# Three float16 products for each float32 projection, and a later first lag product, in a one-core attention and feed-forward kernel

## Chip, cores and metric

The kernel runs on one core of one Trainium2 chip. The metric is the device time of the whole program in microseconds (us), the median of several executions.

## What is computed

The input is x, 4096 rows of 256 channels. Cut to what matters here:

```python
q, k, v = split(layernorm(x) @ Wqkv_w + Wqkv_b)           # 3 x 256 channels, 16 heads of 16
y_softmax = softmax(causal(q @ k.T * scale)) @ v
# a recurrence over all rows, for every head
state = retention * state + Gamma * (v_t outer k_t);  y_t = (W_static + state) @ q_t
g = gelu(layernorm(x) @ gate_w1 + gate_b1)                # 128 channels
alpha = sigmoid(g @ gate_w2 + gate_b2)
x = x + (alpha * y_softmax + (1 - alpha) * y_stp) @ out_w + out_b
x = x + ffn_fp8(layernorm(x))
```

## The kernel before

The kernel has three parts, each a block in which every engine has a program of its own. The engines meet through semaphores, each waits in its own order, and an engine that waits holds up all that stands behind the wait.

**The prologue** makes everything that depends on x alone. x is taken in 8 chunks of 512 rows. For a chunk, VectorE finds mean and variance (`moments`, L830 to L838), GpSimd raises the variance to the power -1/2 (`power`, L584), VectorE normalises (`normalise`, L846), TensorE turns the result so that channels lie on partitions (`turn`, L685), ScalarE copies the turned columns out of PSUM as float32 (`columns`, L769, tile `xn_t`), and TensorE multiplies (`project`, L700): 7 units of 128 output channels (two each for q, k and v, one for the gate), each the sum of two float32 matmuls of 128x128 by 128x512. The units alternate between PSUM banks 2 and 3, so unit u+2 waits until ScalarE has emptied the bank of unit u (`products`, L776, L780, and L785 for the gate's gelu). After that VectorE splits q and k into two float16 parts (`split`, L856 and L858), TensorE turns v back (`turn_back`, L713) and makes the gate's logits (L720), and SyncE (SP) stores all of it in DRAM (`store`, L505, L511, L515) and loads the next x (`next_x`, L497). TensorE's order is project(c), turn(c+1), turn_back(c). VectorE's order, from chunk 0 on, is split(c), moments(c+2), normalise(c+2); for the last chunks it is moments and normalise of chunk c+1, then the maxima of the next paragraph, then split(c).

From chunk 5 on, a first piece of the next part is mixed in: TensorE makes scores of q and k for the first query chunk, pair by pair (`first_maxima`, L664 and L669), between units 2 and 3 of chunk 5 and units 0 to 3 of chunks 6 and 7, and VectorE takes their row maxima (L954). They need q and k of chunks 0 to 3 read back from DRAM: SP waits until these are stored (L560), loads them (L529 and L537) and only then stores chunk 4. The other 22 of the 32 pairs follow behind chunk 7.

At the very start VectorE squares Wqkv (L864), TensorE sums the squares (L728), and a chain of small VectorE instructions with one GpSimd power in it (L599) makes a scale for each channel, to `chan_bias` (L892). Between normalise(1) and split(0) VectorE has a setup chain: constants of the recurrence, and the fp8 rounding of the feed-forward weight (L897 to L946). It waits once for GpSimd's `partition_all_reduce` of one number (L620), behind which GpSimd fills two large tiles (L622, L624).

**The attention part** starts when all engines have left the prologue. Its order of work is written out in a list; `first_steps` (L170) is its beginning: the maxima of the second query chunk (L1232 on TensorE, L1433 on VectorE), 40 pairs through four PSUM banks, and, when 8 single maxima of them have been issued, the first lag product (L1306), a matmul that waits for a GpSimd product `kq` (L1123). **The last part** merges, projects and applies the feed-forward layer.

Of the kernel before, what the change touches and what calls it, by code (L numbers as in the profile page):

```python
# [8 lines left out]
I32 = mybir.dt.int32  # L9
# [26 lines left out]
SHIFT_UNIT = 2.0 ** 15  # L36
SCALE = HD ** -0.5
# [60 lines left out]
N_WEIGHTS = 12  # L98
# [70 lines left out]
def first_steps():  # L169
# [167 lines left out]
def preln_attention_ffn_kernel(nc, x, wqkv, bqkv, out_w, out_b, w_static, lam, gamma, gate_w1,  # L337
                               gate_b1, gate_w2, gate_b2, ffn_wt, ffn_b, out):
    ctx = ExitStack()
    with ctx:  # L340
# [56 lines left out]
        xnt_evac = free_sem("xnt_evac", 2)  # L397
# [61 lines left out]
        with pro:  # L459
# [26 lines left out]
            xn_t = sb("xn_t", [P, 2, HALF, CH], where=pro)  # L486
# [6 lines left out]
            with nc.Block() as block:  # L493
                @block.sync
                def _(sp):
# [46 lines left out]
                    def copy_sides():  # L542
                        sp.wait_ge(pool_setup, 13)
# [36 lines left out]
                def _(pool):  # L580
# [12 lines left out]
                    pool.wait_ge(pool_setup, 5)  # L593
                    power(1)

# [8 lines left out]
                    pool.wait_ge(pool_setup, 8)  # L604
# [7 lines left out]
                    pool.wait_ge(pool_setup, 11)  # L612
# [10 lines left out]
                    pool.wait_ge(pool_setup, 13)  # L623
# [25 lines left out]
                def _(pe):  # L649
# [26 lines left out]
                    pe.wait_ge(pool_setup, 3)  # L676
                    pe.wait_ge(first_weights, 16 * 2)
# [11 lines left out]
                    def project(it, par, between=()):  # L689
# [40 lines left out]
                    mm.then_inc(bounds_ready, 1)  # L730
                    turn(0, 0)
                    pe.wait_ge(weights_loaded, 16 * N_WEIGHTS)
# [16 lines left out]
                def _(act):  # L749
                    for dst, src in [(wqkv_sb[:, :, :], wqkv.rearrange("(c p) n -> p c n", p=P)), (bqkv_sb[:, :], bqkv)]:  # L750
                        act.dma_start(dst, src).then_inc(first_weights, 16)
                    for dst, src in [
                            (w1_sb[:, :, :], gate_w1.rearrange("(c p) n -> p c n", p=P)),
# [10 lines left out]
                    def columns(it, par):  # L764
                        for c in range(HALF):
# [3 lines left out]
                            act.activation(xn_t[:, par, c, :], PS[:, c, :], ACT.Identity).then_inc(xnt_evac, 1)  # L769

                    def products(it, par):

                        act.wait_ge(stored[par], it * STORES_PER_CHUNK + STORES_PER_CHUNK)
                        for u in range(4):
                            act.wait_ge(proj_ready, it * 14 + par * 7 + u + 15)
                            act.activation(proj[:, par, u, :], PS[:, PROJ_BANK + u % 2, :], ACT.Identity,  # L776
                                           bias=chan_bias[:, u:u + 1], scale=chan_scale[:, u:u + 1]).then_inc(proj_evac, 1)
                        for u in range(4, 6):
                            act.wait_ge(proj_ready, it * 14 + par * 7 + u + 15)
                            act.activation(proj[:, par, u, :], PS[:, PROJ_BANK + u % 2, :], ACT.Identity,  # L780
                                           bias=bqkv_sb[:, u:u + 1]).then_inc(proj_evac, 1)
# [3 lines left out]
                        act.activation(gate_t[:, par, :], PS[:, PROJ_BANK + (UNITS_PER_CHUNK - 1) % 2, :], ACT.Gelu, bias=b1_sb[:, 0:1])\  # L785
# [14 lines left out]

                    act.wait_ge(weights_loaded, 16 * N_WEIGHTS)
                    act.activation(lam_sb[:, :], lam_sb[:, :], ACT.Exp, scale=-1.0).then_inc(act_setup, 1)
                    columns(0, 0)

                    act.wait_ge(vaug_ready, 2)
                    act.wait_ge(scales_ready, 7)
# [16 lines left out]
                def _(dve):  # L823
# [26 lines left out]
                    def split(it, par):  # L850
# [10 lines left out]

                    moments(0, 0)
                    dve.wait_ge(first_weights, 16 * 2)
                    dve.tensor_tensor(w_square[:, :, :], wqkv_sb[:, :, 0:2 * D], wqkv_sb[:, :, 0:2 * D], ALU.mult)\  # L864
                        .then_inc(scales_ready, 1)
                    dve.tensor_tensor(bounds[:, :], bqkv_sb[:, 0:4], bqkv_sb[:, 0:4], ALU.mult).then_inc(scales_ready, 1)
                    normalise(0, 0)

# [992 lines left out]
```

## Time and profile before

| | |
|---|---|
| median of 3 executions | 1790.21 us (1789.45 to 1790.47) |
| the profiled execution | 1787.12 us |
| its span, first to last instruction | 1785.4 us |
| TensorE busy | 1645.4 us, 92% |
| VectorE busy | 1524.5 us, 85% |
| ScalarE busy | 1389.0 us, 78% |
| GpSimd busy | 1188.1 us, 67% |
| mean granted TensorE clock | 0.951 |

All times below are of the profiled execution, counted from the first instruction of its span. PE is TensorE, PEld its weight loads, DVE VectorE, ACT ScalarE, POOL GpSimd, SP SyncE; a q behind a name is the engine's sequencer, which issues transfers. A float32 matmul of the program is two matmul records in the trace.

### The profile page before, as it was taken

The numbers are of one execution on the slowest core, as the hardware profiler recorded it, in microseconds if no ns is written. First come the engines' busy times: TensorE is split into PE (matmuls) and PEld (weight loads), VectorE is DVE, ScalarE is ACT, GpSimd is POOL, SyncE is SP. The second block draws the span as 40 slices with busy tenths as digits, with TensorE's granted clock in tenths as the row PEclk, the third lists the DMA queues.
The fourth block names the chain that finished last, engine by engine and source line by source line (L and its number), as shares of the span: only waits on it lengthen the run. The fifth ranks groups of instructions, "written<-read, shape, count | busy, mean of one in ns | idle before, by whom it ended". The sixth has DMA issues, their size and how long they took to land. (4 is left out here: it accounts for less than half of the span.)

```text
span 1785.4 us, 44481 instructions
## 1 busy us (share of the span) xinstructions
PE 1645.4 (92%) x17464; PEld 595.0 (33%) x17464; DVE 1524.5 (85%) x1717; ACT 1389.0 (78%) x2835; POOL 1188.1 (67%) x1138
## 2 busy tenths in 40 slices
PE   7996599999999999999999999999999999997845
PEld 4542123233333332233333333333333233333622
DVE  6557989999899999998999999989999999821877
ACT  3551279998988899989888988898889889997333
POOL 3102397778777777787777777877788889850720
PEclk9996589999999999999999999999999999999965
DMA  4773352232212422332124222321242230201702
GB/s 143 268 247 123 75 128 71 73 83 79 73 64 86 110 68 79 78 79 76 63 83 110 66 84 73 82 77 64 78 121 82 66 96 29 78 8 51 245 12 82
DMA packets 115345, 163.19 MB, mean 91 GB/s; under 512 B 30081, under 2 KB 57793, under 8 KB 115137
## 3 DMA queue, kind: packets, MB, share of 16 engines
q1 hardware_dynamic: 112608, 158.74, 30.5%
q8 instruction: 135, 2.21, 0.5%
q10 hardware_dynamic: 2528, 1.64, 0.3%
q14 instruction: 74, 0.60, 0.1%
HBM read 121.87 MB, written 38.01 MB: 90 GB/s over the span
## 5 line engine op out<-in xcount | busy, mean ns | idle before, releaser
L1433 DVE TENSOR_REDUCE pmax<-PS 128x2 f32<-128x1024 f32 (+2 forms) x1120 | 1204.9, 1130 | 86.8 <-PE PS L1232 65.4
L1386 ACT ACTIVATE probs<-PS 128x512 f32<-128x512 f32 (+3 forms) x2304 | 1149.4, 576 | 159.3 <-PE PS L1270 80.2
L1297 PE MATMUL PS<-probs,V_g 128*17 128x256 f32 (+3 forms) x5064 | 395.9, 385 | 4.1 <-ACT o_t L1407 3.7
L1140 POOL TENSOR_TENSOR v_exp<-v_exp,k_rows 128x512 f32<-128x512 f32 x256 | 321.8, 1284 | 26.7 <-DMA v_exp<-qkv_t 26.6
L1270 PE MATMUL PS<-Q_st,K_st 50*128 50x512 f16 (+3 forms) x1408 | 289.0, 365 | 7.9 <-ACT probs L1386 6.5
L1182 POOL TENSOR_TENSOR state<-odd,q_rows 128x514 f32<-128x514 f32 x256 | 281.7, 1132 | 6.1
L1232 PE MATMUL PS<-K_st,Q_st 48*128 48x512 f16 (+3 forms) x1408 | 272.9, 357 | 0.2
L1297 PE MATMUL PS<-probs,V_first 128*17 128x256 f32 (+2 forms) x3296 | 265.4, 394 | 2.2 <-ACT o_t L1407 2.2
L1270 PE MATMUL PS<-Q_st,K_first 50*128 50x512 f16 (+3 forms) x896 | 194.3, 379 | 11.0 <-ACT probs L1386 5.1
L1232 PE MATMUL PS<-K_first,Q_st 48*128 48x512 f16 (+1 forms) x832 | 179.1, 392 | 18.8 <-DVE pmax L1433 18.5
L1171 POOL COPY carry<-odd 128x4 f32<-128x4 f32 x64 | 12.0, 187 | 256.8 <-DVE odd L1468 256.8
L1270 PEld LDWEIGHTS PS<-Q_st,K_st 50*128 50x128 f16 x1408 | 80.5, 93 | 295.0 <-ACT probs L1386 241.0
L1150 POOL TENSOR_TENSOR pairs<-pairs,v_exp 128x512 f32<-128x512 f32 x128 | 162.6, 1291 | 0.0
L1297 PEld LDWEIGHTS PS<-probs,V_g 128*17 128x17 f32 x5064 | 84.3, 95 | 185.8 <-issue 110.8
L1395 ACT ACTIVATE pairs<-v_exp,decay 128x256 f32<-128x256 f32 x256 | 129.0, 544 | 11.7 <-POOL v_exp L1140 11.7
L1270 PEld LDWEIGHTS PS<-Q_st,K_first 50*128 50x128 f16 x896 | 52.0, 93 | 208.3 <-ACT probs L1386 157.3
L1297 PEld LDWEIGHTS PS<-probs,V_first 128*17 128x17 f32 x3296 | 55.0, 96 | 144.1 <-issue 89.4
L1176 POOL TENSOR_TENSOR odd<-odd,pairs 128x512 f32<-128x512 f32 x64 | 96.6, 1510 | 5.0
L1468 DVE TENSOR_TENSOR_SCAN odd<-decay_x,sums 128x516 f32<-128x516 f32 x64 | 81.6, 1275 | 10.0 <-POOL sums L1161 10.0
L700 PE MATMUL PS<-xn_t,wqkv_sb 128*128 128x512 f32 x192 | 88.5, 610 | 0.9 <-ACT xn_t L769 0.8
L1161 POOL TENSOR_TENSOR sums<-sums,pairs 128x512 f32<-128x512 f32 x64 | 82.8, 1294 | 5.0
L1330 PE MATMUL PS<-state,sum_e 128*32 128x256 f32 x1024 | 77.6, 394 | 0.0
(170 smaller groups left out, 1471.5 us busy)
## 6 DMA issues: line engine op xcount, KB each, us to landing
v_exp<-qkv_t SPq DMA_DIRECT2D x256, 256.0 KB
qkv_t<-proj SPq DMA_DIRECT2D x24, 512.0 KB, 4.2
qk_parts<-parts SPq DMA_DIRECT2D x16, 512.0 KB, 5.6
Q_st<-qk_parts SPq DMA_DIRECT2D x192, 32.0 KB, 3.9
v_rows<-vaug SPq DMA_DIRECT2D x8, 544.0 KB, 6.5
xin<-x SPq DMA_DIRECT2D x8, 512.0 KB, 6.5
k_rows<-qkv_t SPq DMA_DIRECT2D x16, 256.0 KB, 4.1
q_rows<-qkv_t SPq DMA_DIRECT2D x16, 256.0 KB, 6.6
```

Of the source, the lines that this page charges most:

```text
L700: mm = pe.matmul(PS[:, PROJ_BANK + u % 2, :], w, xn_t[:, par, c, :], start=(c == 0), stop=(c == HALF - 1))
L1140: pool.tensor_tensor(v_exp[:, n % RING], v_exp[:, n % RING], k_rows[:, b % 2], ALU.mult)\
L1150: pool.tensor_tensor(pairs[:, B % 2, k:k + 2], pairs[:, B % 2, k:k + 2], v_exp[:, slot:slot + 2, 1:CH:2], ALU.add).then_inc(pair_made, 1)
L1161: pool.tensor_tensor(own[:, :, 1:], own[:, :, 1:], pairs[:, B % 2, :, 1:PAIR:2], ALU.add)\
L1176: pool.tensor_tensor(middle, middle, pairs[:, B % 2, :, 0:PAIR:2], ALU.add).then_inc(middle_made, 1)
L1182: pool.tensor_tensor(state[:, B % STATES, k].rearrange("p (c e) -> p c e", e=PLACES), own[:, k, 0:PAIR + 1].unsqueeze(2).broadcast_to([P, ...
L1232: mm = pe.matmul(PS[:, bank, 0:width], Q_st[rows, c, pair, j * P:(j + 1) * P], keys[rows, pair, blk * CH:blk * CH + width], start=True, st ...
L1270: mm = pe.matmul(PS[:, bank, 0:CH - r * P], keys[rows, pair, kt * P:(kt + 1) * P], Q_st[rows, c, pair, r * P:CH], start=True, stop=(kt < T ...
L1297: mm = pe.matmul(PS[h * VW:h * VW + VN, out_bank(g, s), first:end], v[:, kt, h * VN:(h + 1) * VN], probs[:, tile % P_SLOTS, h, first - r * ...
L1386: act.activation(probs[:, tile % P_SLOTS, h, 0:CH - r * P], PS[:, step[5], 0:CH - r * P], ACT.Exp, scale=SCORE_SCALE).then_inc(exp_done, 1)
L1395: act.activation(pairs[:, B % 2, s % BATCH, :], v_exp[:, s % RING, 0:CH:2], ACT.Identity, scale=decay[:, 0, col:col + 1]).then_inc(u_scale ...
L1433: dve.tensor_reduce(pmax[:, s % 2, pair * TPC + j:GH * TPC:PAIRS * TPC, blk], PS[:, bank:bank + SIDES, 0:width], AX.X, ALU.max).then_inc(m ...
```

## The change

Weights and normalised columns are split into a high and a low float16 part, after multiplying the columns by 1024 and the weights by a power of two that is made from the largest weight. A unit is then the sum of six float16 matmuls (high by high, high by low and low by high, for two halves of the channels) in place of two float32 ones. The scale for undoing this is folded into the instructions that empty PSUM. The largest weight is found by VectorE and by a new `partition_all_reduce` on GpSimd. ScalarE makes the high parts and the squares of the weights. VectorE makes the low parts, among them `low_columns` for every chunk, behind `split` in its order, and `project` waits for it. `ones` is made by VectorE and gate_w1 is loaded earlier. In the attention part the first lag product stands behind 20 single maxima in place of 8.

```diff
 # first_steps
         if release and n == 8:
             steps.append(release)
+        if s > 0 and n == MAXES[s] // 4:
             steps += [("lag", 0, 0, 2), ("lag_evac", 0, 0, 2)]
 # tiles
-            xn_t = sb("xn_t", [P, 2, HALF, CH], where=pro)
+            xn_t = sb("xn_t", [P, 2, 2, HALF, CH], F16, where=pro)
+            w_parts = sb("w_parts", [P, 2, HALF, 3 * D], F16, where=pro)
+            w1_parts = sb("w1_parts", [P, 2, HALF, GATE], F16, where=pro)
 # GpSimd
-                    pool.memset(ones[:, :], 1.0).then_inc(pool_setup, 1)
...
                     power(1)
+                    pool.wait_ge(peak_found, 3)
+                    pool.partition_all_reduce(w_peak[:, 3:4], w_peak[:, 2:3], P, bass.bass_isa.ReduceOp.max)\
+                        .then_inc(peak_spread, 1)
 
                     for par in range(2):
                         pool.memset(vaug[...], 1.0).then_inc(vaug_ready, 1)
                     pool.wait_ge(bounds_ready, 2)
                     pool.tensor_tensor(ratio[:, :], ratio[:, :], quarter[:, :], ALU.pow).then_inc(bounds_ready, 1)
 # TensorE
-                    pe.wait_ge(pool_setup, 3)
-                    pe.wait_ge(first_weights, 16 * 2)
+                    pe.wait_ge(squared, 1)
...
+                            if u == 4:
+                                pe.wait_ge(w_split, 3)
                             for c in range(HALF):
-                                w = wqkv_sb[:, c, u * P:(u + 1) * P] if u < 6 else w1_sb[:, c, :]
-                                mm = pe.matmul(PS[:, PROJ_BANK + u % 2, :], w, xn_t[:, par, c, :],
-                                               start=(c == 0), stop=(c == HALF - 1))
+                                for n, (w_part, x_part) in enumerate(SPLIT_PRODUCTS):
+                                    w = w_parts[:, w_part, c, u * P:(u + 1) * P] if u < 6 else w1_parts[:, w_part, c, :]
+                                    mm = pe.matmul(PS[:, PROJ_BANK + u % 2, :], w, xn_t[:, par, x_part, c, :],
+                                                   start=(c == 0 and n == 0),
+                                                   stop=(c == HALF - 1 and n == len(SPLIT_PRODUCTS) - 1))
 # ScalarE
-                            act.activation(xn_t[:, par, c, :], PS[:, c, :], ACT.Identity).then_inc(xnt_evac, 1)
+                            act.activation(xn_t[:, par, 0, c, :], PS[:, c, :], ACT.Identity, scale=X_GAIN).then_inc(xnt_high, 1)
...
+                    act.wait_ge(first_weights, 16 * 3)
+                    act.activation(w_square[:, :, :], wqkv_sb[:, :, 0:2 * D], ACT.Square).then_inc(squared, 1)
                     act.activation(lam_sb[:, :], lam_sb[:, :], ACT.Exp, scale=-1.0).then_inc(act_setup, 1)
+                    act.wait_ge(unit_ready, 3)
+                    act.activation(w_parts[:, 0, :, 0:2 * D], wqkv_sb[:, :, 0:2 * D], ACT.Identity, scale=w_unit[:, 2:3])
                     columns(0, 0)
+                    act.activation(w_parts[:, 0, :, 2 * D:3 * D], ...)
+                    act.activation(w1_parts[:, 0], w1_sb[:, :, :], ...)
 # VectorE
+                    def low_columns(it, par):
+                        for c in range(HALF):
+                            dve.wait_ge(xnt_high, it * 4 + par * 2 + c + 1)
+                            dve.scalar_tensor_tensor(out=xn_t[:, par, 1, c, :], in0=PS[:, c, :], scalar=X_GAIN,
+                                                     in1=xn_t[:, par, 0, c, :], op0=ALU.mult, op1=ALU.subtract)\
+                                .then_inc(xnt_evac, 1)
...
                     moments(0, 0)
-                    dve.tensor_tensor(w_square[:, :, :], ...)
+                    dve.tensor_reduce(w_peak[:, 0:1], wqkv_sb ..., apply_absolute_value=True).then_inc(peak_found, 1)
+                    dve.tensor_reduce(w_peak[:, 1:2], w1_sb ..., apply_absolute_value=True).then_inc(peak_found, 1)
+                    dve.tensor_reduce(w_peak[:, 2:3], w_peak[:, 0:2], AX.X, ALU.max).then_inc(peak_found, 1)
                     normalise(0, 0)
+                    dve.wait_ge(peak_spread, 1)
+                    # five instructions of one column: w_unit
                     # the chain of bounds, to ratio
+                    low_weights(w_parts[:, 1, :, 0:2 * D], wqkv_sb[:, :, 0:2 * D], w_parts[:, 0, :, 0:2 * D], 1)
                     dve.wait_ge(bounds_ready, 3)
                     # chan_scale, chan_bias
+                    dve.tensor_scalar(chan_gain[:, :], chan_scale[:, :], w_unit[:, 3:4], None, ALU.mult)
+                    low_columns(0, 0)
+                    low_weights(w_parts[:, 1, :, 2 * D:3 * D], ..., 2)
+                    low_weights(w1_parts[:, 1], w1_sb[:, :, :], w1_parts[:, 0], 3)
                     moments(0, 1)
...
                     with dve.Fori(0, NCH // 2 - 2) as it:
                         for par in range(2):
                             split(it, par)
+                            low_columns(it + par, 1 - par)
                             moments(it + 1, par)
                             normalise(it + 1, par)
                     for c in range(NCH - 4, NCH):
...
                         split(c // 2, c % 2)
+                        if c + 1 < NCH:
+                            low_columns((c + 1) // 2, (c + 1) % 2)
```

## Rows read from the trace of the kernel before

**Rows 1.** Stretches: start and us, busy of PE, PEld, DVE, ACT, POOL, clock, DMA share, GB/s.

```profile
34.60:143.80 109.20, 108.26 (x388) 55.58 (x389) 60.41 (x107) 60.03 (x105) 9.67 (x18) 1.00 0.73 238
143.80:168.10 24.30, 12.62 (x69) 3.25 (x68) 23.30 (x22) 0.22 (x1) 0.00 (x0) 0.57 0.30 102
168.10:218.40 50.30, 26.57 (x116) 6.44 (x116) 44.47 (x48) 5.75 (x10) 23.35 (x20) 0.50 0.43 104
```

**Rows 2.** Timeline of TensorE (start, us, instruction): where the chunks' projections begin.

```profile
17.83 11.96 PE L700 MATMUL PS<-xn_t,wqkv_sb 128*128 128x512 f32 x24 [0.77 <-ACT xn_t L769]
...
34.63 10.57 PE L700 MATMUL PS<-xn_t,wqkv_sb 128*128 128x512 f32 x24
...
46.75 1.04 PE L685 MATMUL PS<-ident,xn 128*128 128x128 f32 x8
...
49.35 10.55 PE L700 MATMUL PS<-xn_t,wqkv_sb 128*128 128x512 f32 x24
...
64.74 10.57 PE L700 MATMUL PS<-xn_t,wqkv_sb 128*128 128x512 f32 x24
...
94.84 5.42 PE L700 MATMUL PS<-xn_t,wqkv_sb 128*128 128x512 f32 x12
...
110.61 1.96 PE L700 MATMUL PS<-xn_t,wqkv_sb 128*128 128x512 f32 x4
...
127.36 1.96 PE L700 MATMUL PS<-xn_t,wqkv_sb 128*128 128x512 f32 x4
```

**Rows 3.** Timeline of TensorE in the last part: four bfloat16 matmuls in a row.

```profile
1730.62 1.89 PE L1650 MATMUL PS<-r_t,wq 128*128 128x512 bf16 x4 [1.20 <-ACT r_t L1695]
```

**Rows 4.** Timeline of ScalarE at the ends of chunks 1 and 2.

```profile
47.03 0.69 ACT L785 ACTIVATE gate_t<-PS,b_sb 128x512 f32<-128x512 f32 x1 [1.11 <-PE PS L700]
47.61 1.08 ACT L769 ACTIVATE xn_t<-PS 128x512 f32<-128x512 f32 x2
...
61.73 1.28 ACT L785 ACT_TABLE_LOAD   x1 [1.10 <-PE PS L700]
```

**Rows 5.** GpSimd's lines L620 and L584: duration ns min/median/max, first and last start us.

```profile
L620 POOLq MODIFY_POOL_CONFIG  x2: 11/11/11, 21.2 to 21.3; - x2
L620 POOL PARTITION_ALL_REDUCE wsmall<-wsmall x1: 377/377/377, 27.2 to 27.2; - x1
...
L584 POOLq MODIFY_POOL_CONFIG  x2: 83/83/83, 33.6 to 33.7; - x2
```

**Rows 6.** Timeline of GpSimd and VectorE at the start.

```profile
11.28 0.28 POOL L588 TENSOR_SCALAR_AFFINE_SELECT ident<-ident 128x128 f32<-128x128 f32 x1 [10.28 <-issue]
...
11.77 1.06 POOL L584 TENSOR_TENSOR rstd<-var_eps,neg_half 128x4 f32<-128x4 f32 x1
...
16.12 0.70 POOL L599 TENSOR_TENSOR ratio<-ratio,quarter 128x2 f32<-128x2 f32 x1 [3.00 <-DVE ratio L880]
...
17.81 1.39 DVE L830 BATCH_NORM_STATS2 stats<-xin 128x6 f32<-128x256 f32 x4
```

**Rows 7.** Timeline of VectorE: setup chain, its end, and moments of chunk 2.

```profile
34.95 0.69 DVE L944 SCALAR_TENSOR_TENSOR wtmp<-wtmp 128x512 f32<-128x512 f32 x1
...
40.18 1.40 DVE L830 BATCH_NORM_STATS2 stats<-xin 128x6 f32<-128x256 f32 x4
```

**Rows 8.** Timeline of VectorE between chunks 5 and 6, and of SP at the early loads.

```profile
107.49 1.40 DVE L830 BATCH_NORM_STATS2 stats<-xin 128x6 f32<-128x256 f32 x4
...
110.75 1.38 DVE L846 TENSOR_SCALAR xn<-xin,mv,rstd 128x256 f32<-128x256 f32 x4 [1.12 <-POOL rstd L584]
...
87.21 2.68 SPq L529 DMA_DIRECT2D Q_st<-qk_parts  x6
89.94 4.32 SPq L537 DMA_DIRECT2D K_first<-qk_parts  x6
```

**Rows 9.** Timeline of the attention part's first steps, TensorE and VectorE.

```profile
176.66 1.22 PE L1306 MATMUL PS<-kq,lag_sum 128*128 128x256 f32 x2 [2.38 <-POOL kq L1123]
...
178.35 21.78 DVE L1433 TENSOR_REDUCE pmax<-PS 128x2 f32<-128x256 f32 x21 [3.00 <-PE PS L1241]
```

More of the change, by code:

```diff
@@ L36 @@
 SHIFT_UNIT = 2.0 ** 15
+X_GAIN = 2.0 ** 10
+W_GAIN = 2.0 ** 13
+SPLIT_PRODUCTS = ((0, 0), (0, 1), (1, 0))
 SCALE = HD ** -0.5
@@ L97 @@
 N_SCALE = 5
-N_WEIGHTS = 12
+N_WEIGHTS = 11
 PAD = 1024
@@ L485, in preln_attention_ffn_kernel @@
             var_eps = sb("var_eps", [P, TPC], where=pro)
-            xn_t = sb("xn_t", [P, 2, HALF, CH], where=pro)
+            xn_t = sb("xn_t", [P, 2, 2, HALF, CH], F16, where=pro)
+            w_parts = sb("w_parts", [P, 2, HALF, 3 * D], F16, where=pro)
+            w1_parts = sb("w1_parts", [P, 2, HALF, GATE], F16, where=pro)
+            w_peak = sb("w_peak", [P, 4], where=pro)
+            w_unit = sb("w_unit", [P, 4], where=pro)
+            chan_gain = sb("chan_gain", [P, 4], where=pro)
             proj = sb("proj", [P, 2, 6, CH], where=pro)
@@ L776, in products @@
                             act.activation(proj[:, par, u, :], PS[:, PROJ_BANK + u % 2, :], ACT.Identity,
-                                           bias=chan_bias[:, u:u + 1], scale=chan_scale[:, u:u + 1]).then_inc(proj_evac, 1)
+                                           bias=chan_bias[:, u:u + 1], scale=chan_gain[:, u:u + 1]).then_inc(proj_evac, 1)
                         for u in range(4, 6):
@@ new lines, in low_weights @@
+                    def low_weights(low, whole, high, made):
+                        dve.wait_ge(w_high, made)
+                        dve.scalar_tensor_tensor(out=low, in0=whole, scalar=w_unit[:, 2:3], in1=high,
+                                                 op0=ALU.mult, op1=ALU.subtract).then_inc(w_split, 1)
+                    dve.memset(ones[:, :], 1.0).then_inc(scales_ready, 1)
+                    moments(0, 0)
+                    dve.wait_ge(first_weights, 16 * 3)
+                    dve.tensor_reduce(w_peak[:, 0:1], wqkv_sb[:, :, :].rearrange("p c n -> p (c n)"), AX.X, ALU.max,
+                                      apply_absolute_value=True).then_inc(peak_found, 1)
@@ new lines, in _ @@
+                    dve.tensor_scalar(w_unit[:, 0:1], w_peak[:, 3:4], 1e-30, None, ALU.max).then_inc(unit_ready, 1)
+                    dve.wait_ge(unit_ready, 1)
+                    dve.tensor_scalar(w_unit[:, 1:2].bitcast(I32), w_unit[:, 0:1].bitcast(I32), EXPONENT_BITS, None,
+                                      ALU.bitwise_and).then_inc(unit_ready, 1)
+                    dve.wait_ge(unit_ready, 2)
+                    dve.reciprocal(w_unit[:, 0:1], w_unit[:, 1:2]).then_inc(peak_found, 1)
@@ L869, in _ @@
+                    dve.wait_ge(peak_found, 4)
+                    dve.tensor_scalar(w_unit[:, 2:3], w_unit[:, 0:1], W_GAIN, None, ALU.mult).then_inc(unit_ready, 1)
+                    dve.tensor_scalar(w_unit[:, 3:4], w_unit[:, 1:2], 1.0 / (W_GAIN * X_GAIN), None, ALU.mult)\
+                        .then_inc(unit_ready, 1)
                     dve.wait_ge(bounds_ready, 1)
@@ L892, in _ @@
                     dve.tensor_tensor(chan_bias[:, :], bqkv_sb[:, 0:4], chan_scale[:, :], ALU.mult).then_inc(scales_ready, 1)
+                    dve.wait_ge(unit_ready, 4)
+                    dve.tensor_scalar(chan_gain[:, :], chan_scale[:, :], w_unit[:, 3:4], None, ALU.mult).then_inc(scales_ready, 1)
+                    low_columns(0, 0)
+                    low_weights(w_parts[:, 1, :, 2 * D:3 * D], wqkv_sb[:, :, 2 * D:3 * D], w_parts[:, 0, :, 2 * D:3 * D], 2)
+                    low_weights(w1_parts[:, 1], w1_sb[:, :, :], w1_parts[:, 0], 3)
                     moments(0, 1)
```

42 lines of the change are left out of this document (26 added, 16 removed).

## The prediction

> **What bounds the kernel now.** I read the stretches first [rows 1]. In chunks 1 to 7 TensorE is busy 108.3 of 109.2 us, at the full clock, while VectorE and ScalarE work about 60 us each: the projections bound this part. Behind it, to 168.1, VectorE is busy 23.3 of 24.3 us with maxima, and to 218.4 it is busy 44.5 of 50.3. So time taken from TensorE in the prologue moves everything that follows, and comes back only where VectorE and its inputs can keep up. The timeline gives the chunks' starts [rows 2]: 17.83 for chunk 0, then 34.63, 49.35, 64.74 (chunk 3), 94.84 (chunk 5), 110.61 and 127.36; the tail starts at 143.8. A plain chunk lasts 14.72 us, of which 12.12 are the 28 projection records and 2.60 the three turning stages; chunk 2 takes 15.4, because ScalarE loads a table of 1.28 us ahead of the gelu [rows 4], and so does chunk 4 (3 and 4 together take 30.1).
>
> **What a unit costs.** Now 4 records in 1.73 us (12.12 / 7). Four bfloat16 matmuls of the same 128x512 took 1.89 us at half the clock [rows 3]: one ends about 0.61 behind its start, so the spacing is (1.89 - 0.61) / 3 = 0.427, and 0.213 at the full clock. Six are 1.28 us, 7 units 8.96 in place of 12.12. ScalarE empties a bank in 0.71 to 0.78 us and two banks alternate, so it just keeps up.
> By the Trainium skill (TensorE: Matmul & The Clock Gate, Back-to-back issue gap) matmuls of 512 columns in a stream with weight loads are about 131 ns apart, not 213; that would make a unit 0.79 us. The row at the half clock shows no such overlap, and the sum stays at 0.213.
>
> **Added to each chunk.** project(c+1) now waits for `low_columns(c+1)`: VectorE's two passes behind ScalarE's. Before, with the projection over at 46.75, the gelu began at 47.03, the copies ended at 48.69 and project began at 49.35, 0.66 later, held by TensorE's own work [rows 2, 4]. Now the gelu with a scale from memory costs 0.09 more, and the last low half starts 0.1 behind the last copy and takes about 0.67 (the same operation from SBUF took 0.69 [rows 7]), with 0.1 to hand over: 2.85 in place of 2.60. With the table load the copies end at once with TensorE's work, so there it is 4.15 in place of 3.29, and a second table load at the chunk's start costs 0.2 as bank 2 is emptied late. A plain chunk: 8.96 + 2.85 = 11.8 (saves 2.9). Chunks 2 and 4: 13.3 (saves 2.1).
>
> **The start.** This is where it is given back. Ahead of the `partition_all_reduce` of L620 stand two MODIFY_POOL_CONFIG at 21.3, and it starts at 27.2: 5.9 us, though VectorE's input was there at 23.1. Behind it the next power (L584) has such a pair again [rows 5]. power(1) ends at 12.83 [rows 6]; exchange to 18.8; the all-reduce is seen by VectorE at about 19.6; exchange back from 19.5 to 25.4; then the power of `ratio`, which started at 16.12 before and now at 25.4. From there VectorE needed 1.69 to its next stage at 17.81 [rows 6], so 27.1, plus 0.2 for `chan_gain`, plus 2 x 0.69 for low_columns(0) and 0.1: project(0) begins at 28.8 to 28.9 in place of 17.83. The two reductions for the largest weight (about 2.2 us, by the 1.22 us that maxima of 1024 columns take) run while GpSimd is still loading and cost nothing; ScalarE's high parts, about 1.1 us, fit in the second exchange. Without that cover they would cost their own length.
> By the Trainium skill (GPSIMD Engine Reference, Instruction dispatch) the first call to a freshly loaded GpSimd kernel pays about 6 us: 11.9 for the two. It is the rule that speaks against the change; the trace has 5.9 here and 10.28 at the kernel's start [rows 6].
>
> Then comes a wait that I take for the dearest. low_columns(1) stands in VectorE's order behind low_weights 2 and 3 (1.1 us), moments(1), normalise(1), the whole setup chain and split(0). VectorE's way from moments(1) at 17.81 to moments(2) at 40.18 is 22.4 us [rows 6, 7]; it was idle to TensorE and now is not. GpSimd's exchange and fills in it move along, so I keep its length. It starts at 29.9: low_columns(1) runs at 52.3 to 53.7, project(1) begins at 53.8 in place of 34.63, 19.2 later. TensorE idles 11 us before it, and begins at half the clock, as it did in chunk 0, where 24 records took 11.96 us and not 10.57 [rows 2]: 1.4 us of chunk 1's gain.
>
> **Chunks 5 to 7.** Chunk 5's maxima need q and k of chunks 0 to 3. SP was released at 87.21 and had issued the loads at 94.26 [rows 8]; they land near 97.6, 10.4 behind. The stores of chunk 3 are bound by the transfers, so by the new starts SP is released near 100.6 and the loads land at 111.0, while TensorE wants them at 109.5: 1.5 us of waiting. Chunk 6: low_columns(6) ends just ahead of project(6), and moments(7) and normalise(7), 4.6 us [rows 8], now stand behind it and ahead of the maxima; TensorE, with one pair of banks, waits for the first of them, 2.6 us. Chunk 7: ScalarE's `decay_x` of 3.7 us now outlasts two short units and costs 1.1; there is no low_columns behind it.
>
> **The sum** of the chunks against 34.63: +19.2; chunk 1 -1.5; 2 -2.1; 3 -2.9; 4 -2.1; 5 -1.4; 6 -0.3; 7 -2.1: +6.9 at the tail. The tail is VectorE's, and moves as a whole.
>
> **The lag product.** TensorE waited 2.38 for `kq`, VectorE then 3.00 [rows 9]. Behind 20 maxima, six pairs or 6.8 us later, `kq` is there. The product (1.2 us) still stands between two pairs, where TensorE has only 0.5 us to spare, so VectorE loses 0.6: -2.4. ScalarE and GpSimd get their work 5 us later, and GpSimd is idle for 27 us after it.
>
> Together +4.5 us: 1787.1 becomes 1791.6 for the profiled execution. That execution stands 3.1 below the median of the runs, so I predict 1794.7. A measurement here can tell about 0.2% (3.6 us) from no change.
>
> **Rivals.** (1) Faster: the exchanges are not on the path, because the compiled program needs one load only, or the second runs while VectorE waits anyway. It decides by the start of project(0): 17 rather than 29. Both gone are 11.8 us: 1783. For it speaks only that the first exchange of the start hides work anyway; against it both pairs in rows 5. 0.12. (2) Slower by more: the transfers. They fill 0.73 of their time at 14.7 us a chunk [rows 1], and at 12 us a chunk and a late start, x(7) and the early keys each land later than TensorE wants them, one us for one us; with an exchange near the 10.3 us of the start it is as much again. About +5: 1800. 0.15. (3) The projection is as short as an emptying ScalarE allows, 0.98 us a unit ((0.79 + 0.30 + 0.87) / 2): 2.1 us less for each of 8 chunks, 1778; the skill's 131 ns above is that rule. The half clock row speaks against it: 0.02. (4) VectorE's chain is shorter than before because its waits for GpSimd fall in other places (one instruction of it waits out the fills): up to 4 us less, 1791, no change that can be told. 0.13. My own case has 0.58.
>
> **Range and chances.** Unknown prices: an exchange 5.9 to 10.3 (and 0 if not needed), low half 0.64 to 0.9, the waits of chunks 5 and 6 0 to 6, the lag 0 to 3.0. I take the near rows for the centre, and 1786 to 1802 as the range, which leaves out the first and third rival. Slower by over 0.2% is the upper two thirds of my own case and the second rival: 0.55; the rest of it and the fourth are within 0.2%: 0.29; faster 0.16.
>
> **What would show it.** In the profile after: two pairs of MODIFY_POOL_CONFIG before the power of ratio, and project(0) near 29; TensorE idle from about 42 to 54, ended by VectorE's low part; then chunks of 11.8 and 13.3 us; a wait for the keys in chunk 5 and for a maximum in chunk 6; the tail near 151; VectorE idle under 1 us at the lag product. I am wrong if project(1) begins before 45, or if a plain chunk takes over 13.

## The result, and the profile after

The changed kernel takes 1798.28 us (median of 4 executions, 1798.01 to 1800.25) against 1789.99 us for the kernel before (4 executions): a ratio of 1.0046, 95% interval 1.0034 to 1.0058. It is slower by 8.3 us, where 4.5 were forecast. The profiled execution took 1798.01 us, with a span of 1796.2: 10.8 us more than the profiled execution of before, which was one of the shorter ones. All that follows compares these two traces, so it has 10.8 to explain.

The start, on TensorE (start, us, instruction, idle time before it and what ended it):

```profile
14.24 1.95 PE L697 MATMUL PS<-ident,xn 128*128 128x128 f32 x8
29.53 11.40 PE L715 MATMUL PS<-xn_t,w_parts 128*128 128x512 f16 x42 [13.34 <-DVE xn_t L892]
...
53.90 6.42 PE L715 MATMUL PS<-xn_t,w_parts 128*128 128x512 f16 x20 [9.61 <-DVE xn_t L892]
```

These answer to the first two lines of [rows 2]. project(0) begins 11.7 us later than before (17.83), project(1) 19.27 us later (34.63). From there the trace gives the starts of the later projections, and the tail's first maximum on VectorE:

```profile
67.91 9.24 PE L715 MATMUL PS<-xn_t,w_parts 128*128 128x512 f16 x42 [0.24 <-DVE xn_t L892]
...
81.19 10.93 PE L715 MATMUL PS<-xn_t,w_parts 128*128 128x512 f16 x42 [0.70 <-DVE xn_t L892]
...
94.87 9.24 PE L715 MATMUL PS<-xn_t,w_parts 128*128 128x512 f16 x42 [0.16 <-DVE xn_t L892]
...
108.16 5.75 PE L715 MATMUL PS<-xn_t,w_parts 128*128 128x512 f16 x18 [0.70 <-DVE xn_t L892]
...
122.72 1.47 PE L715 MATMUL PS<-xn_t,w_parts 128*128 128x512 f16 x6 [0.17 <-DVE xn_t L892]
...
129.41 0.24 PE L677 MATMUL PS<-K_first,Q_st 48*128 48x128 f16 x2 [3.49 <-DVE pmax L1016]
129.47 0.37 PE L682 MATMUL PS<-mask_qk_sides,ident_sides 64*128 64x128 bf16 x4
129.78 2.74 PE L715 MATMUL PS<-xn_t,w_parts 128*128 128x512 f16 x6
...
141.47 1.47 PE L715 MATMUL PS<-xn_t,w_parts 128*128 128x512 f16 x6
```

```profile
155.91 10.34 DVE L1016 TENSOR_REDUCE pmax<-PS 128x2 f32<-128x1024 f32 x10 [1.61 <-PE PS L677]
```

Set against the starts in [rows 2] and VectorE's first tail maximum at 144.22 in the trace of before, the delay runs as follows. The right-hand columns are what each chunk gave back.

| at | before | after | delay | measured | forecast |
|---|---|---|---|---|---|
| project(1) | 34.63 | 53.90 | +19.27 | | +19.2 |
| project(2) | 49.35 | 67.91 | +18.56 | -0.71 | -1.5 |
| project(3) | 64.74 | 81.19 | +16.45 | -2.11 | -2.1 |
| project(5) | 94.84 | 108.16 | +13.32 | -3.13 (two chunks) | -5.0 |
| project(6) | 110.61 | 122.72 | +12.11 | -1.21 | -1.4 |
| project(7) | 127.36 | 141.47 | +14.11 | +2.00 | -0.3 |
| tail | 144.22 | 155.91 | +11.69 | -2.42 | -2.1 |
| first scan | 218.29 | 228.44 | +10.15 | -1.54 | -2.4 |

A unit takes 1.295 us and its six matmuls are 9.07 / 42 = 0.216 us apart at the full clock (9.07 being from the start of project(2) at 67.91 to the next turn at 76.98). So the products themselves did what the forecast had them do, and the table's misses lie elsewhere: chunks 1, 3, 6 and the lag product. What the three chunks have in common is seen in the stretches of TensorE alone (start and us, busy, granted clock, DMA share, GB/s):

```profile
79.00:82.00 3.00, 1.93 (x12) 0.96 0.15 40
82.00:85.00 3.00, 3.00 (x9) 0.50 0.92 335
85.00:88.00 3.00, 3.00 (x15) 0.97 1.05 402
...
126.00:129.00 3.00, 0.00 (x0) 1.00 1.08 379
129.00:132.00 3.00, 2.60 (x12) 0.59 0.41 148
```

A granted clock of 0.50 is the lower of the two levels, 1.2 GHz of 2.4. It comes behind the wait at 81.19 and behind the one at 129.41, and also at the start of project(5) (0.68 from 108 to 111). Before, the granted clock was 1.00 from 34.60 to 143.80 [rows 1].

In chunk 3 VectorE, too, waits, for x(4), the rows of chunk 4, whose load SP issues only at 79.79, behind twelve small transfers:

```profile
84.56 1.41 DVE L857 BATCH_NORM_STATS2 stats<-xin 128x6 f32<-128x256 f32 x4 [3.43 <-DMA xin<-x]
```

TensorE doesn't feel this wait here, since the low clock makes project(3) longer; it does in e6_fill below.

GpSimd at the start: its timeline, and then the same lines' instructions with the code exchange (duration ns min/median/max, first and last start us).

```profile
11.51 1.06 POOL L595 TENSOR_TENSOR rstd<-var_eps,neg_half 128x4 f32<-128x4 f32 x1
18.52 0.38 POOL L606 PARTITION_ALL_REDUCE w_peak<-w_peak  x1 [5.96 <-issue]
...
26.25 0.73 POOL L612 TENSOR_TENSOR ratio<-ratio,quarter 128x2 f32<-128x2 f32 x1 [7.08 <-issue]
```

```profile
L606 POOLq MODIFY_POOL_CONFIG  x2: 11/11/11, 12.8 to 12.8; - x2
...
L612 POOLq MODIFY_POOL_CONFIG  x2: 86/86/86, 19.0 to 19.1; - x2
```

The pairs of MODIFY_POOL_CONFIG are there as [rows 5] had them, once in each direction. Towards the all-reduce GpSimd stands still for 5.96 us and towards the power for 7.08. The first fits the Trainium skill (GPSIMD Engine Reference, Instruction dispatch), which gives about 6 us for the first call to freshly loaded code; the way back is 1.1 us dearer here than the way there.

And VectorE's setup chain, in two pieces:

```profile
27.02 0.34 DVE L940 TENSOR_SCALAR ratio<-ratio 128x2 int32<-128x2 int32 x1 [4.85 <-POOL ratio L612]
...
30.37 1.39 DVE L857 BATCH_NORM_STATS2 stats<-xin 128x6 f32<-128x256 f32 x4
...
40.84 5.53 DVE L1002 TENSOR_SCALAR wtmp<-ffnw_sb,wsmall 128x512 f32<-128x512 f32 x1
46.40 0.43 DVE L1003 TENSOR_SCALAR wtmp<-wtmp 128x512 int32<-128x512 int32 x1
...
49.09 1.23 DVE L883 CAST parts<-proj 128x2048 f16<-128x2048 f32 x1 [0.34 <-DVE wq L1008]
50.35 2.29 DVE L885 TENSOR_TENSOR parts<-proj,parts 128x2048 f16<-128x2048 f32 x1
52.56 1.28 DVE L892 SCALAR_TENSOR_TENSOR xn_t<-PS,xn_t 128x512 f16<-128x512 f32 x2
```

From moments(1) at 30.37 VectorE never waits longer than 1.14 us, and low_columns(1) is the last of it. One line stands out: L1002 takes 5.53 us for 128x512 while the like instruction behind it, L1003, takes 0.43. The kernel before had the same (5.11 us at 28.88, its L940), inside a chain that nobody waited for.

### The profile page after: what moved, and what is told of

Same layout as the page of the kernel before. It is cut to its first block and busy times, and to the rows that moved or that the text cites. A ratio compares the mean times of both kernels' runs of the same rounds, so it can differ in the third digit from the quotient of the medians.

```text
span 1796.2 us, 44756 instructions
## 1 busy us (share of the span) xinstructions
PE 1628.8 (91%) x17576; PEld 585.1 (33%) x17576; DVE 1538.7 (86%) x1745; ACT 1394.2 (78%) x2839; POOL 1189.4 (66%) x1138
## 5 line engine op out<-in xcount | busy, mean ns | idle before, releaser
L715 PE MATMUL PS<-xn_t,w_parts 128*128 128x512 f16 x336 | 84.4, 411 | 26.0 <-DVE xn_t L892 24.9
```

## Experiments

My theory was: 19 us come from a path at the start that goes GpSimd's two exchanges, VectorE's setup chain, low_columns(1), project(1); the chunks keep their lengths, so whatever is taken off this path arrives at the tail. Rivals: the transfers bound the chunks and swallow it, or the delay is in some other link. Besides the ratios I compare the start of VectorE's first scan in each profiled run (218.29 before, 228.44 after), which is all of the prologue and the first maxima and free of what scatters later. Each is one execution, and they differ without a cause in the code: GpSimd's first power starts between 11.48 and 12.30 in the changed kernel and its variants, and e2_lag_back, which has the changed kernel's code up to the tail, reached the tail 0.85 us earlier (155.06 against 155.91), mostly because chunk 1 took 13.39 us and not 14.01. A difference under about 1 us between two starts shows nothing by itself.

| run | ratio to before (95%) | project(0) | project(1) | first scan |
|---|---|---|---|---|
| before | | 17.83 | 34.63 | 218.29 |
| changed kernel | 1.0046 (1.0034 to 1.0058) | 29.53 | 53.90 | 228.44 |
| e1_lag_only | 0.9993 (0.9984 to 1.0002) | 17.30 | 34.31 | 216.46 |
| e2_lag_back | 1.0055 (1.0042 to 1.0069) | 29.69 | 54.11 | 229.15 |
| e3_spread_matmul | 1.0002 (0.9993 to 1.0011) | 20.77 | 45.16 | 218.54 |
| e4_columns_early | 1.0040 (1.0026 to 1.0053) | 29.25 | 50.34 | 225.20 |
| e5_power_first | 1.0039 (1.0026 to 1.0053) | 27.59 | 52.24 | 226.25 |
| e6_fill | 1.0055 (1.0043 to 1.0067) | 29.92 | 54.29 | 229.35 |
| e7_fills_act | 1.0030 (1.0019 to 1.0041) | 28.91 | 48.30 | 223.05 |
| e8_best | 0.9966 (0.9953 to 0.9979) | 21.37 | 38.62 | 211.68 |
| e9_x7_early | 1.0042 (1.0028 to 1.0055) | 30.42 | 54.71 | 228.46 |
| e10_best_x7 | 0.9951 (0.9938 to 0.9965) | 21.27 | 38.52 | 210.96 |

### The lag product by itself, and taken back

```diff
 # the kernel before, first_steps
             steps.append(release)
+        if s > 0 and n == MAXES[s] // 4:
             steps += [("lag", 0, 0, 2), ("lag_evac", 0, 0, 2)]
```

The second run does the reverse to the changed kernel.

> The kernel before with only the later lag product. My theory: TensorE's wait for kq (2.38 us) and most of VectorE's 3.00 us go, VectorE keeps a loss of 0.6 to 1.8 us at the product; nothing ahead of it moves. 1.5 to 2.4 us faster than before. Rival: ScalarE's and GpSimd's work behind the product comes later and is waited for at the scan: no gain, or up to 1 us slower.

> The changed kernel with the lag product back behind 8 maxima. My theory: the two parts of the change are independent, so it stands 9.8 to 10.7 us over before (the change's 8.3 plus 1.5 to 2.4), with the waits for kq back (2.4 us on TensorE, 3.0 on VectorE) and the tail's start at 155.5 as in the changed kernel. Rival (the lag part is worth nothing): 8.3 over before.

TensorE and VectorE at the product, in the kernel before with the later lag product:

```profile
180.50 1.22 PE L1307 MATMUL PS<-kq,lag_sum 128*128 128x256 f32 x2
```

```profile
182.30 16.00 DVE L1434 TENSOR_REDUCE pmax<-PS 128x2 f32<-128x1024 f32 x15 [1.79 <-PE PS L1233]
```

TensorE's wait for `kq` is gone, and VectorE's 3.00 us [rows 9] have become 1.79. From the tail's first maximum to the first scan it is 72.55 us (143.91 to 216.46) in place of 74.07. Taken back in the changed kernel it is 74.09 (155.06 to 229.15) in place of 72.53. Both traces say 1.5 us. The median of the first run is 1788.16 against 1790.14, but the interval of its ratio reaches 1.0002: by times alone the gain isn't shown, by the traces it is.

### The largest weight without GpSimd

```diff
-                    pool.wait_ge(peak_found, 3)
-                    pool.partition_all_reduce(w_peak[:, 3:4], w_peak[:, 2:3], ...)
 # VectorE, behind the peak of each partition
+                    dve.tensor_scalar(peak_diag[:, :], ident[:, :], w_peak[:, 2:3], None, ALU.mult)
 # TensorE, behind the sums of squares; ones_sq is 128x128
+                    pe.matmul(PS[:, 5, 0:P], ones_sq[:, :], peak_diag[:, :], start=True, stop=True)
 # VectorE
+                    dve.tensor_reduce(w_peak[:, 3:4], PS[:, 5, 0:P], AX.X, ALU.max)
```

> The changed kernel with the largest weight spread over the partitions by one TensorE product (ones by a diagonal of the 128 peaks) and one VectorE maximum, so that GpSimd runs its powers without an exchange between them. My theory: w_unit near 16 us, the power of ratio near 17, project(0) at 20.3 in place of 29.5, project(1) at 44.7 in place of 53.9, and the tail 9 us earlier, since the chunks keep their lengths: 1789, 0 to 2 us under before. Rival (transfers bound the chunks: stores, early keys and x(7) do not come 9 us earlier): project(0) is as early, but chunks 5 and 6 wait for keys and x, and 3 to 5 us of it is lost: 1793. Second rival (the code exchange is paid anyway at the next power): project(0) is not before 26.

```profile
12.30 1.14 POOL L598 TENSOR_TENSOR rstd<-var_eps,neg_half 128x4 f32<-128x4 f32 x1
...
16.67 0.70 POOL L612 TENSOR_TENSOR ratio<-ratio,quarter 128x2 f32<-128x2 f32 x1 [2.94 <-DVE ratio L944]
```

Two powers with no exchange between them: the second waits for VectorE and for nothing else. project(0) begins 8.76 us earlier than in the changed kernel, project(1) 8.74 earlier, and the first scan 9.90 earlier. The extra 1.2 us are in chunk 1 (13.51 in place of 14.01, no more than executions of the same code differ) and in chunk 6 (18.06 in place of 18.75; VectorE waits 0.23 us for x(7) there and not 0.90). The ratio is 1.0002. So the exchanges put about 9 us on the path, nearly as much as the whole net loss of 10, and what is taken off arrives at the first scan: the transfers take nothing of it. project(1) still stands 10.5 us behind the kernel before (45.16 against 34.63); that part is VectorE's chain.

### One exchange in place of two on the path

```diff
 # GpSimd: power of ratio first, then the all-reduce of the peak
-                    pool.partition_all_reduce(w_peak[:, 3:4], w_peak[:, 2:3], ...)
...
                     pool.tensor_tensor(ratio[:, :], ratio[:, :], quarter[:, :], ALU.pow)
+                    pool.wait_ge(peak_found, 3)
+                    pool.partition_all_reduce(w_peak[:, 3:4], w_peak[:, 2:3], ...)
 # VectorE: the chain of bounds ahead of that of w_unit
```

> The changed kernel with the power of ratio and VectorE's chain of bounds ahead of the new all-reduce, so that one exchange of GpSimd's code lies on the way to project(0) and the exchange back falls where GpSimd waits for VectorE. My theory (each exchange is a fixed 6 to 7 us, paid only where the kind of GpSimd instruction changes): the power of ratio starts near 15.5 us in place of 26.3, the all-reduce near 22, project(0) at 26.2 in place of 29.5, and with it project(1) and the tail 3.3 us earlier: 1795. Rival (the exchange back is now waited for at rstd(1) and the next one at the second all-reduce, as they follow each other closely): project(0) is earlier, project(1) is not: 1798.

```profile
15.31 0.70 POOL L609 TENSOR_TENSOR ratio<-ratio,quarter 128x2 f32<-128x2 f32 x1 [1.88 <-DVE ratio L924]
21.73 0.38 POOL L611 PARTITION_ALL_REDUCE w_peak<-w_peak  x1 [5.72 <-issue]
...
31.01 1.05 POOL L595 TENSOR_TENSOR rstd<-var_eps,neg_half 128x4 f32<-128x4 f32 x1 [7.23 <-DVE var_eps L865]
```

The theory holds, the size does not: project(0) is 1.94 earlier, not 3.3. GpSimd's first power started 0.57 later in this execution (12.08 against 11.51), and the high parts of the weights (ScalarE, 1.15 us, waited for 1.16 by VectorE) had been hidden in the second exchange and no longer are. The exchange back, 7.23 us, now ends only with rstd(1): VectorE waits for it 1.54 us where it waited 1.14. The first scan is 2.19 us earlier.

### The setup chain, the fills, and the third link

```diff
 # e4_columns_early, VectorE: five instructions of the setup chain go behind
+                    split(0, 0)          # and left out of the loop behind
+                    low_columns(0, 1)
                     link(dve.tensor_scalar(wtmp[:, 0], ffnw_sb[:, :], wsmall[:, 4:5], FP8_MAX, ...))
 # e7_fills_act: GpSimd's two fills go to ScalarE, ahead of its wait for chan_gain
-                    pool.memset(K_first[:, :, :], SHIFT_UNIT)
-                    pool.memset(sum_e[:, :, :, :, :], 0.0)
+                    act.activation(K_first[:, :, :], fill_of[:, 0:1] (broadcast), ACT.Identity)
+                    act.activation(sum_e[...], fill_of[:, 1:2] (broadcast), ACT.Identity)
```

> The changed kernel with split(0) and low_columns(1) moved ahead of the last five instructions of VectorE's setup chain (the rounding of the feed-forward weight). My theory: the wait of TensorE for low_columns(1) is only VectorE's order; split starts at 41.0, low_columns(1) ends near 46, project(1) begins at 46 in place of 53.9, and with a shorter idle stretch the low clock behind it is shorter too: the tail 8 us earlier, 1790. Rival: the 5.5 us of the first rounding instruction (128x512, beside GpSimd's fill of a large tile) is a delay of whatever VectorE instruction stands there, so split takes it over: project(1) at 50 to 51, tail 3 to 4 us earlier, 1794 to 1795.

> The changed kernel with GpSimd's two large fills (4.43 and 1.87 us) made by ScalarE, which waits for chan_gain from 22.8 to 28.5 us then and from 45.3 on. My theory, after the run with split(0) ahead: VectorE's instruction beside GpSimd's fills does not get on until these end, so without them the first rounding instruction takes 0.5 in place of 5.5 us, project(1) begins at 48.9 in place of 53.9 and the tail is 5 us earlier: 1793. Rival: the 5.5 us come from something else that the trace does not show (what VectorE reads, for instance) and stay: 1798.

With split(0) moved ahead, VectorE and, below it, GpSimd:

```profile
40.42 6.33 DVE L883 CAST parts<-proj 128x2048 f16<-128x2048 f32 x1
46.79 2.29 DVE L885 TENSOR_TENSOR parts<-proj,parts 128x2048 f16<-128x2048 f32 x1
49.00 1.28 DVE L892 SCALAR_TENSOR_TENSOR xn_t<-PS,xn_t 128x512 f16<-128x512 f32 x2
50.20 0.48 DVE L1004 TENSOR_SCALAR wtmp<-ffnw_sb,wsmall 128x512 f32<-128x512 f32 x1
```

```profile
39.41 4.43 POOL L635 MEMSET K_first<- 128x5120 f16 x1
43.72 1.87 POOL L637 MEMSET sum_e<- 128x2048 f32 x1
45.46 0.22 POOL L638 MEMSET decay_x<- 128x32 f32 x1
```

The rival was right. The CAST took 1.23 us in the changed kernel and takes 6.33 here, from 40.42 to 46.75; the rounding instruction, which had 5.53, has 0.48. Whichever instruction VectorE has there does its own 1.23 or 0.48 us of work only when GpSimd's second large fill is over, at 45.6. project(1) comes 3.56 us earlier and not 8. With the fills on ScalarE the same rounding instruction takes 0.48:

```profile
40.29 0.48 DVE L1009 TENSOR_SCALAR wtmp<-ffnw_sb,wsmall 128x512 f32<-128x512 f32 x1
40.81 0.43 DVE L1010 TENSOR_SCALAR wtmp<-wtmp 128x512 int32<-128x512 int32 x1
```

project(1) begins 5.60 us earlier and the first scan 5.39, with nothing else touched; 5.05 of it are this instruction. By the Trainium skill (SBUF — State Buffer, Who interferes with whom) the port pair that VectorE and GpSimd share is an exclusive lock, and a VectorE copy, cast or tensor_scalar in its two-port mode is held up entirely while GpSimd has it. The trace agrees (0.48 becomes 5.53, 1.23 becomes 6.33), and it adds that VectorE did not get its turn between the two large fills. Not every VectorE instruction is held up: in the changed kernel four of one column, from 40.06 to 40.80, ran in 0.15 or 0.16 us each while the first fill (39.83 to 44.26) was on.

### Filling TensorE's gaps

```diff
 # TensorE; discarded 128x512 products into a free bank
+                    def filler(par, count):
+                        for _ in range(count):
+                            pe.matmul(PS[:, 5, :], w_parts[:, 0, 0, 0:P], xn_t[:, par, 0, 0, :], start=True, stop=True)
 # project, ahead of its wait for low_columns: 3 in chunks 1, 3 and 5
+                        filler(1 - par, fill)
 # turn_back, ahead of its wait for gate_t: 2 in chunks 0, 2 and 4
+                        filler(par, fill)
```

> The changed kernel with two discarded 128x512 products ahead of the wait for the gelu in chunks 0, 2 and 4 and three ahead of the waits of project(1), (3) and (5) for low_columns. TensorE's records at these places show 0.49 and 0.70 us of waiting, which they fill (0.2157 us each). My theory: the half clock for 3.4 us at the start of project(3) and project(5) follows these gaps; with them filled the granted clock stays full, each of the two projections takes 9.1 in place of 10.8 us, tail 3.4 us earlier: 1795. Rival: the half clock has nothing to do with the gaps: the projections stay at 10.8, the time is the same or up to 0.5 us longer.

```profile
79.00:82.00 3.00, 2.94 (x23) 1.00 0.11 24
82.00:85.00 3.00, 2.96 (x15) 1.00 0.61 205
85.00:88.00 3.00, 3.00 (x16) 1.00 1.05 409
```

```profile
95.23 9.24 PE L720 MATMUL PS<-xn_t,w_parts 128*128 128x512 f16 x42 [1.05 <-DVE xn_t L898]
...
115.28 0.39 PE L677 MATMUL PS<-K_first,Q_st 48*128 48x512 f16 x2 [2.70 <-issue]
```

For chunks 3 and 5 the cause is confirmed: with the gaps filled the granted clock stays at 1.00, project(3) takes 9.24 in place of 10.93 us, and the first 18 products of project(5) take 4.06 in place of 5.75. Ahead of project(1), where 8.20 us of waiting are left, the three products help nothing: its projection had 11.77 us (11.01 in the changed kernel).

The gain isn't shown: the first scan is 0.91 us later. This execution had lost 1.15 us by project(2), before the first filled gap that worked; from there to the tail it is 0.24 us shorter than the changed kernel, which is less than executions differ. What the clock gave back was taken by two other waits. At project(4) TensorE waits 1.05 us for VectorE (0.16 before), so of 1.69 us chunk 3 gives back 0.79 (12.89 in place of 13.68): VectorE had waited 3.35 us for x(4) (to 85.64), and normalise(4), split(3) and then low_columns(4) follow in its order. In chunk 5 the first maxima wait 2.70 us: SP had begun to issue the key loads at 107.18, 1.29 later than in the changed kernel, and TensorE asks for them near 112.6. The profile names no releaser for this wait; that it is the keys is my reading of the loads, the last of which is issued at 109.5 and took up to 5.7 us to land. This is the wait for keys that the forecast had; the low clock had only covered it.

Waits of this size are not enough by themselves. In e8_best and e10_best_x7 the same two waits of 0.49 and 0.69 us stand ahead of project(1), and the clock did not fall. In e8_best:

```profile
38.62 9.24 PE L715 MATMUL PS<-xn_t,w_parts 128*128 128x512 f16 x42 [0.69 <-DVE xn_t L899]
```

```profile
40.00:43.00 3.00, 3.00 (x16) 1.00 1.03 342
```

Ahead of project(3) and project(5) of the same two runs it fell as in the changed kernel (10.76 us for the projection of chunk 3). What else it takes isn't shown.

### All repairs of the start together, and x(7)

> The three together: largest weight spread by TensorE, split(0) and low_columns(1) ahead of the last five setup instructions, large fills on ScalarE. My theory (all three are waits on one path and add up, and the chunks behind keep their lengths): project(0) at 20.8, split(0) at 32.3, project(1) at 37.3 in place of 53.9, tail at 139 in place of 155.5 (before: 143.8): 1781 to 1783, 0.4 to 0.5% under before. Rival (transfers bound the chunks once the start is early): project(1) is as early, but chunks 5 and 6 wait for keys and x(7), and the tail is at 142 or later: 1785 to 1788.

> The changed kernel with the load of x(7) issued by SP before its wait for the stores of chunk 3 (near 99 us in place of 114.0), and moments(7) and normalise(7) directly behind those of chunk 6, ahead of chunk 5's maxima. My theory: TensorE's 3.49 us of waiting for a maximum in chunk 6, and the half clock behind it, come from VectorE making chunk 7's columns there at the wrong moment. Moved, they cost about 2 us at chunk 5's maxima, where keys are nearly waited for anyway, and give back 3.5 us plus 1.3 to 1.7 us of clock in chunk 6: tail 2.5 to 3.5 us earlier, 1795 to 1796. Rival: the work is 3.7 us of VectorE wherever it stands and the maxima of chunk 5 pay it in full, or x(7) delays the keys: same time, 1798.

> The kernel with all three repairs of the start, with the same two moves of x(7) and of moments(7) and normalise(7). My theory: independent of the start, so again 2.5 to 3.5 us less than without them: 1780 to 1781, 0.5% under before. Rival: as for the same moves alone, no gain: 1783.7.

```diff
 # e9_x7_early and e10_best_x7, SP
                     next_x(NCH // 2 - 2, 0)
+                    next_x(NCH // 2 - 2, 1)
                     for par in range(2):
                         sp.wait_ge(stored[par], STORES_PER_CHUNK * (1 + (c + 2 - par) // 2))
...
-                    next_x(NCH // 2 - 2, 1)
 # VectorE: moments and normalise of chunks 6 and 7 one behind the other, ahead of chunk 5's maxima
```

The three repairs of e8_best leave project(1) at 38.62, 15.3 us earlier than in the changed kernel, and the first scan 16.76 earlier; 1783.67 us, ratio 0.9966 (0.9953 to 0.9979), faster than both kernels. I had 37.3, and 16.5 at the tail; the difference at project(1) is that ScalarE, busy with the fills until 25.8, lets TensorE wait 1.26 us in project(0), and its columns for chunk 1 come 1.07 late. In chunk 5 the first maxima wait 0.35 us, so nearly all of the transfers is still hidden.

The move of x(7) in the changed kernel does nothing that can be told. The first scan is at 228.46, 228.44 without it, though project(1) came 0.81 us later in this execution. Chunks 5 and 6 together take 32.70 us, and 32.74 on top of e8_best, where the changed kernel and the six variants with these chunks unchanged took 32.62 to 33.61. Chunk 6 loses its wait, and chunk 5 gets it:

```profile
119.02 0.39 PE L677 MATMUL PS<-K_first,Q_st 48*128 48x512 f16 x2 [2.64 <-DVE pmax L1016]
119.35 5.75 PE L715 MATMUL PS<-xn_t,w_parts 128*128 128x512 f16 x18
...
127.85 1.47 PE L715 MATMUL PS<-xn_t,w_parts 128*128 128x512 f16 x6 [0.17 <-DVE xn_t L892]
```

The wait of 2.64 us is followed by 18 matmuls in 5.75 us, 4.06 at the full clock, so the low clock came along with the wait. My figure of 2.5 to 3.5 us was wrong because it took the clock's part for a saving. On top of e8_best the first scan is 0.72 earlier and the ratio 0.9951 (0.9938 to 0.9965); the two were timed on different occasions, and their intervals overlap, so only the step from the changed kernel and from the one before is certain.

## Why the prediction was right, and where its sum was off

**Sign and place: right.** The change is slower, and by more than 0.2%, which the prediction gave 0.55, and the reasons given are the ones at work. The first rival (no exchange on the path) is out: project(0) begins at 29.53 and not at 17. *The exchanges*: forecast 5.9 each on the path, measured 5.96 and 7.08; without them project(0) is 8.8 us earlier, and all of it reaches the first scan. *project(0)*: "begins at 28.8 to 28.9", measured 29.53; the excess is the way back. *project(1)*: "begins at 53.8 in place of 34.63", measured 53.90. VectorE's chain kept its length (from moments(1) at 30.37 to low_columns(1) at 52.56 it is 22.2, forecast 22.4). 5 of these us are VectorE held up by GpSimd's fills, as the fourth rival had it ("one instruction of it waits out the fills"); but the fills stood behind the same instruction as before, so that rival, a shorter chain, did not come. What I had not seen is that the hold-up follows the fills to whatever stands beside them.

**The unit: right.** 0.213 forecast for the spacing, 0.216 measured; the 131 ns of the Trainium skill (TensorE: Matmul & The Clock Gate, Back-to-back issue gap) are not seen, nor a unit bound by ScalarE (third rival).

**The chunks: the step that failed.** The prediction had 8.96 + 2.85 = 11.8 for a plain chunk. No chunk of the changed kernel was under 13.2, and none of a variant under 12.4. Chunks 2 and 4, with the table load, came out at 13.28 and 13.29, as forecast (13.3). Chunks 1 and 3 took 14.01 and 13.68. Chunk 3's projection alone had 10.76 in place of 9.07 us (81.19 to 91.95), since TensorE began it at 1.2 GHz. The forecast let the clock fall only where TensorE idles for 11 us, ahead of chunk 1. It also fell behind a turning stage with waits of 0.49 and 0.70 us in it, and behind 3.49 us in chunk 6. So the term put at nothing is the low clock in chunk 3, 1.7 us, most of the missed 1.9 us of chunks 3 and 4. The rest of the 11.8 stands: 13.68 less 1.69 of clock and 0.16 of waiting for VectorE is 11.83. But no run had such a chunk. With the clock up chunk 3 took 12.89 (e6_fill) and chunk 1 12.47 (e8_best), 1.05 and 0.64 us of them waits for a VectorE that was late for other reasons, x(4) in the one and the setup instructions moved behind low_columns(1) in the other; the prediction had put such waits at nothing, too. Chunk 1 missed by 0.8: its projection took 11.01 where 1.4 us of loss made it 10.4. In e2_lag_back, the same code, it took 10.39, so this miss is no more than executions differ. The prediction's own sign of being wrong, a plain chunk over 13, did appear, then.

The half clock in chunk 0, which the prediction read from 11.96 us in place of 10.57, is not in the granted clock, which stands at 1.00 there in every run, also where the records of the changed kernel's project(0) come at half the pace (6 of them from 29 to 32 us). At the start the pace has to be read from the records.

**Chunk 5: right in sum, by another cause.** 1.5 us were to be spent waiting for keys. In their place stood the low clock; filled, the wait for keys appeared, at 2.70.

**Chunk 6: too small.** Forecast 2.6 us of waiting, measured 3.49, because x(7) landed late (VectorE waits 0.90 for it), and then 1.3 us of low clock on the unit behind it (2.74 in place of 1.47). Together they are 2.2 of the 2.3 us that this row is off.

**The lag product: mis-sized.** 2.4 us forecast, 1.5 measured in two pairs of traces (before and e1_lag_only, e2_lag_back and the changed kernel). VectorE still loses 1.79 us at the product where I had 0.6: the product has 1.2 us of it, and the rest is, I take it, what TensorE needs to fill the banks again.

**The size: partly luck.** Tail +11.69 in place of +6.9 (the prediction's own terms add up to 6.8), lag -1.5 in place of -2.4, so +10.15 in place of +4.5 at the first scan. Between the two medians only 8.3 are left of it; the profiled execution of before stood 2.9 below its median and that of after at the low end of its own, 0.3 below. That offset was in the forecast, added on top; what the difference between medians has less than that between spans, I can't assign to a place. Between the two traces the forecast is off by more than half (10.8 against 4.5); that it stands closer to the medians is no merit of the sum.

**Second rival (transfers).** Not the cause of the loss at the start: they take nothing from e3_spread_matmul or e7_fills_act. They have small parts in it, x(7) in chunk 6, and they are the next bound: with the clock repaired, x(4) holds up chunk 3 and the keys chunk 5 (e6_fill).

**Open.** Why the exchange back takes 1.1 us longer than the one forth wasn't tried. Nor was what kept the clock up ahead of project(1) in e8_best. Nor was a way to empty VectorE's list between split(5) and the maxima of chunk 6, which neither place for chunk 7's moments does.

## What to carry to other kernels

A change that shortens the products of a stage by a quarter still lost, because what it needs first (one number across the partitions, low halves behind a setup chain) was put on the path to the first product. Count the switches between kinds of GpSimd work ahead of the first matmul, and use a TensorE product with ones for a single maximum: here that alone was worth 9 us. When a newly critical chain holds an instruction ten times longer than its like, look at what the other engine does at that moment before moving anything. And a stage made shorter must have its gaps counted too: a few tenths of waiting may cost more in granted clock than in waiting, but filling them pays only if nothing else is late next, as x(4) and the keys were here.

## What the runs showed of the hardware that I had not expected

- VectorE's two instructions of 0.48 and 1.23 us took 5.53 and 6.33 beside GpSimd's fills of 4.43 and 1.87 us and did not slip in between the two. In e8_best ScalarE made the same fills in 4.46 and 1.90 us, and VectorE was not held up. One-column instructions of 0.15 us ran beside the first fill unhindered.
- The exchange of GpSimd's code from the all-reduce back to the power took 6.60 to 7.46 us in the changed kernel and the five variants that keep its order there, the one forth 5.68 to 6.04.
- The granted clock fell to 1.2 GHz behind waits as short as 0.49 and 0.70 us, among small products of the turning stage, and stayed at 2.4 GHz when five discarded products stood in those waits. Each of these falls cost a projection 1.7 us. It did not fall behind waits of 0.49 and 0.69 us ahead of project(1) in e8_best and e10_best_x7.
